# Four transposes of a graph network moved from TensorE to VectorE, a scratch tensor and DMA, and the weights loaded in four groups

## The reference, cut to what matters

```python
# layer 0
h1, h2, h3 = x @ W1, x @ W2, x @ W3
e = leaky_relu(h1 @ h2.T, 0.2); e = where(adj > 0, e, NEG)
x = layernorm(x + relu(softmax(e) @ h3))
# layer 1
h = x @ W; e = leaky_relu(h@a1 [:, None] + h@a2 [None, :]); e = where(adj > 0, e, NEG)
x = layernorm(x + elu(softmax(e) @ h))
# layer 2: a perceptron, an unmasked attention ("mixing"), a perceptron, a masked attention ("hand")
out = relu(x @ mlp1_w + mlp1_b)                     # 512 wide
out = elu(elu(softmax(f1[:, None] + f2[None, :]) @ h_fc)) + out
out = relu(out @ mlp2_w + mlp2_b)                   # 256 wide, the mixed output "o3"
out = relu(elu(elu(attention(out, adj, W_hand, a_hand))) + out)
x = layernorm(x + out)
# layer 3: four heads, adjacency mask
x = layernorm(x + (softmax(mask(q @ k.T / 8)) @ v) @ wo.T + bo)
```

## Time and profile before

| | |
|---|---|
| median of 3 runs | 2919.27 us (2908.69 to 2920.22) |
| the profiled execution, its own time | 2918.28 us |
| its span, first to last instruction | 2916.5 us |
| PE, PEld, DVE, ACT, POOL busy, share of the span | 92, 87, 78, 69, 53% |
| mean granted TensorE clock | 0.983 of full |
| instructions | 61536 |

### The profile page before, as it was taken

One profiled execution on the slowest core, in us unless ns is written; L12 is line 12 of the kernel. 1 busy time (PEld: TensorE's weight loads), 2 busy tenths in 40 slices (PEclk: granted clock), 3 DMA queues, 4 the chain that ended last, 5 costly groups with the idle time before them and its releaser, 6 DMA issues.

```text
span 2916.5 us, 61536 instructions
## 1 busy us (share of the span) xinstructions
PE 2689.4 (92%) x22472; PEld 2551.3 (87%) x22472; DVE 2278.2 (78%) x6124; ACT 1998.7 (69%) x4801; POOL 1556.0 (53%) x2119
## 2 busy tenths in 40 slices
PE   4689999999999999999999999999999999999974
PEld 4589999999999999998999998999999999998863
DVE  3257888888888888888888887888888888888874
ACT  1357777777777776777777777777777777776752
POOL 0235555555555555555556555555655555555542
PEclk9799999999999999999999999999999999999997
DMA  3001222222122122212212221221222122122222
GB/s 109 19 16 37 77 81 64 57 81 80 41 80 81 59 63 80 74 47 81 80 51 71 81 72 49 81 81 48 74 81 70 52 80 80 41 81 73 66 66 73
DMA packets 132766, 195.17 MB, mean 67 GB/s; under 512 B 14832, under 2 KB 97136, under 8 KB 132464
## 3 DMA queue, kind: packets, MB, share of 16 engines
q1 hardware_dynamic: 132464, 191.24, 22.7%
HBM read 107.30 MB, written 83.89 MB: 66 GB/s over the span
## 4 chain that ended last, share of the span: by engine, by line
PE 60%; DMA 13%; ACT 8%; SPq 8%; DVE 6%; issue 4%; POOL 1%; POOLq 0%; DVEq 0%
PE ps L224 29%; DMA p4T<-scratch 10%; PE ps L378 6%; SPq L208 6%; PE ps L240 5%; PE ps L436 4%; PE ps L337 4%; PE ps L233 3%; PE ps L338 3%; DMA scratch<-p 3%; DVE p L950 3%; PE ps L456 2%; ACT p L671 2%; PE ps L360 2%; DVE h_lo L692 1%
## 5 line engine op out<-in xcount | busy, mean ns | idle before, releaser
L1067 POOL TENSOR_TENSOR p<-p,rd 128x512 f32<-128x512 f32 x256 | 269.8, 1054 | 20.0
L671 ACT ACTIVATE p<-p,nmx 128x256 f32<-128x256 f32 x512 | 255.7, 504 | 25.4 <-DVE nmx L935 25.2
L991 POOL TENSOR_TENSOR o1Tp_lo<-o1T,o1Tp_hi 128x1024 fp32r<-128x1024 f32 x64 | 153.8, 2403 | 220.8 <-ACT o1Tp_hi L472 220.8
L1003 POOL TENSOR_SCALAR xn<-act,nmean,rstd 128x256 f32<-128x256 f32 x384 | 243.6, 643 | 18.3 <-POOL rstd L998 11.2
L456 PE MATMUL ps<-p4T,v 128*64 128x256 f32 x1024 | 144.3, 404 | 118.2 <-DMA p4T<-scratch 117.7
L995 POOL TENSOR_TENSOR vare<-mv,eps 128x2 f32<-128x2 f32 x256 | 108.0, 422 | 270.5 <-DVE mv L748 270.5
L1060 POOL TENSOR_TENSOR rd<-some,den 128x2 f32<-128x2 f32 x256 | 53.5, 209 | 354.6 <-DVE den L944 354.6
L456 PEld LDWEIGHTS ps<-p4T,v 128*64 128x64 f32 x1024 | 67.3, 140 | 178.1 <-DMA p4T<-scratch 96.5
L692 DVE TENSOR_TENSOR xnT_lo<-ps,xnT_hi 128x512 fp32r<-128x512 f32 x192 | 132.1, 688 | 114.2 <-ACT xnT_hi L472 114.2
L935 DVE CUSTOM_DVE_ANT_0 p<-ps,mask 128x256 f32<-128x256 f32 x512 | 189.9, 418 | 33.3 <-PE ps L436 33.3
L480 ACT ACTIVATE sco<-sco,nmax 128x256 f32<-128x256 f32 x384 | 191.0, 500 | 28.9 <-DVE nmax L736 28.9
(11 more groups left out here) (248 smaller groups left out, 12683.1 us busy)
## 6 DMA issues: line engine op xcount, KB each, us to landing
scratch<-p SPq DMA_DIRECT2D x128, 512.0 KB, 2.9
p4T<-scratch SPq DMA_DIRECT2D x512, 128.0 KB, 3.9
x0T<-in_xT SPq DMA_DIRECT2D x64, 256.0 KB, 4.6
x<-in_x SPq DMA_DIRECT2D x64, 256.0 KB, 3.7
out<-xn SPq DMA_DIRECT2D x64, 256.0 KB, 3.0
o1T<-in_mlp SPq DMA_DIRECT2D x1, 512.0 KB, 4.4
p<-in_mlp SPq DMA_DIRECT2D x1, 512.0 KB, 4.5
att<-in_fc SPq DMA_DIRECT2D x1, 512.0 KB, 5.4
```

Of the source, the lines that this page charges most:

```text
L671: ins = nc.scalar.activation(rows_, rows_, ACT.Exp, scale=-1.0, bias=nmx4[:, h, m:m + 1], accum_out=den4[:, h, m:m + 1])
L991: return G.tensor_tensor(lo, whole, hi.bitcast(fp32), ALU.subtract)
L1003: ins = G.tensor_scalar(xn[:, m, :], y[:, m, :], nmean[i][:, m:m + 1], rstd[i][:, m:m + 1], ALU.add, ALU.mult)
L1067: G.tensor_tensor(rows_, rows_, rd4[:, h, :].unsqueeze(2).unsqueeze(3).broadcast_to([P, NT, QUADS, CT * QP]), ALU.mult).then_inc(S["p4n"], 1)
```

## The change

- **Turns.** `t0`, `t1`, `t3` and `o3` leave TensorE. DVE transposes 32 by 32 blocks of the tile (`turn`, `V.transpose`, 128x512) into `act[i]` (or `sco[2]` for the mixed output), SP writes it to a scratch tensor (one DMA of 256 KB, packets of 2 KB) and reads it back with four DMAs of 64 KB (packets of 512 B). ACT then makes the high part and POOL the low part from SBUF, in a block order (`high_of_turned`, `low_of_turned`). `r3` adds the turned mixed output from SBUF in two instructions.
- **Column sums.** `d2` has a stationary of 128 columns of ones, so the sums stand in every partition at once: 4 matmuls of 256 columns. DVE takes the reciprocal of 256 columns straight to `rdb`. The two spreading transposes and ACT's copy go.
- **Scores of layers 1 and 3** are written by ACT to SBUF (`sco`) and not to PSUM; DVE masks them there. `pfc` likewise.
- `n4` moves from DVE to POOL, with one `xn3` buffer instead of two. PSUM banks are handed over by a table of tenants.
- **Loads** come in four groups. Only W1, W2, W3, the first x and adj stand ahead of the first product; the splitting of the other weights is called from `run` on DVE just before the first use.
- The five lists of `ORDERS` are new, their highest stage is 8 instead of 9; `l0` is in stage 0 instead of 1.

```diff
@@ ORDERS (pe, first entries and the part around a4; the others are new as well)
-    "pe": "h3:8 a0:3 v4:9 f3:8 x0:5 g0:2 s40:9 d2:7 x1:6 t3:8 s42:9 v2:7 a3:8 m2:6 h0:2 b2:7 n2:6 o3:8 w2:7 s0:2 h1:5 c2:6 f1:5 t0:2 a4:9 r2:6 t1:5 ...",
+    "pe": "g0:0 c2:4 a1:3 h1:2 r2:4 a3:6 a0:1 f2:4 f1:2 a4:7 m3:5 y4:7 x1:3 h0:0 x3:6 m2:3 s0:0 q4:6 k4:6 h3:5 n2:3 v4:6 f3:5 d2:4 s40:6 v2:4 w2:4 s42:6 x0:1",
+    "sp": "i42:8 o5:6 o1:3 lt:0 i1:3 o0:1 i5:6 o3:6 st:8 i0:1 i3:6 o40:7 lx:1 o42:7 i40:7",
@@ sync
+            def pro_out(i):
+                def step(t):
+                    sp.wait_ge(S[f"pro{i}_x"], t + 1)
+                    wait(sp, S[f"pro{i}_dma"], back(t - 1))
+                    sp.dma_start(scratch_pro[i].rearrange("p w n -> p (w n)"), flat(act[i])).then_inc(S[f"pro{i}_dma"], 16)
+            def pro_in(i):
+                def step(t):
+                    sp.wait_ge(S[f"pro{i}_dma"], sent(t))
+                    for w in range(QUADS):
+                        sp.dma_start(rows_[w * QP:(w + 1) * QP, :, :], scratch_pro[i][:, w, :].rearrange("(q j) n -> j q n", q=QUADS)).then_inc(...)
@@ tensor
-            def t0(t):
-                pe.wait_ge(S["pro0"], t + 1)
-                transposes(bank[0], sco[0]).then_inc(S["proT0_mm"], 1)
             def d2(t):
                 pe.wait_ge(S["pfcl"], t + 1)
-                for m in range(NT):
-                    for k in range(NT):
-                        for i in (1, 0):
-                            ins = nc.tensor.matmul(ps[:, 5, 2 * m:2 * m + 2], pfcp[i][:, k, m * P:(m + 1) * P], ones2[:, :], ...
+                enter(5, "rdb", t + 1)
+                for k in range(NT):
+                    for i in (1, 0):
+                        ins = nc.tensor.matmul(ps[:, 5, 0:N], ones2[:, :], pfcp[i][:, k, :], ...
-            def b2(t):
-                pe.wait_ge(S["rdc"], t + 1)
-                spread(ps[:, 5, N:2 * N], lambda m: rdc[:, m:m + 1]).then_inc(S["b2_mm"], 1)
@@ scalar
             def t0(t):
-                ac.wait_ge(S["proT0_mm"], t + 1)
-                copy(proT[0][0][:, :, :], bank[0]).then_inc(S["proT0h"], 1)
+                ac.wait_ge(S["pro0_dma"], back(t))
+                wait(ac, S["av0_mm"], t)
+                high_of_turned(proT[0], 0).then_inc(S["proT0h"], 1)
@@ vector
+            def turn(i):
+                blocks = sco[i][:, :, :, :].rearrange("p b a n -> p (b a) n").rearrange("p c (w j) -> p w c j", w=QUADS)
+                return V.transpose(flat(act[i]).rearrange("p (w c j) -> p w c j", w=QUADS, j=QP), blocks)
             def t0(t):
-                dv.wait_ge(S["proT0h"], t + 1)
-                low_part(proT[0], bank[0]).then_inc(S["proT0"], 1)
+                dv.wait_ge(S["pro0"], t + 1)
+                wait(dv, S["xn0"], t)
+                turn(0).then_inc(S["pro0_x"], 1)
             def d2(t):
                 dv.wait_ge(S["d2_mm"], t + 1)
-                V.reciprocal(rdc[:, :], ps[:, 5, 0:4:2]).then_inc(S["rdc"], 1)
+                wait(dv, S["att"], t)
+                V.reciprocal(rdb[:, :], ps[:, 5, 0:N]).then_inc(S["rdb"], 1)
@@ gpsimd
+            def t0(t):
+                po.wait_ge(S["proT0h"], t + 1)
+                low_of_turned(proT[0], 0).then_inc(S["proT0"], 1)
```

561 lines of the change are left out of this document (335 added, 226 removed), and 8 rows, old and new, of the table ORDERS.

## The result

The changed kernel takes **2988.11 us** (median of 4 runs, 2986.22 to 2990.06), the kernel before 2916.61 us in the same session (2908.69 to 2920.22). The ratio is 1.0232 with a 95% interval of 1.0205 to 1.0259: 2.3% slower, where 3.4% faster was forecast.

A forecast was written before the change was run, and what follows sets the result against it. PE was taken as the bound: 38.67 us of work plus 2.4 of wait, 41.1 a round. 14.5 + 245 + 55 x 41.1 + 299 = 2819 us, plus 1.8 outside the span: 2820 us; 8 in 10 from 2725 to 2905.

The forecast's parts named there:

- Neither binds: Claim that DVE, at 36.8 us in a round of 41.1, and POOL, at 29.6, would not limit the kernel.
- What the others gain: Work on engines other than PE per round: DVE 35.1 to 39.5 us, taken as 36.8; ACT near 31; POOL 29.6.
- my upper bound of 39.5: Most DVE work expected per round, with SBUF inputs costing 3.0 us and the wide reciprocal adding 1.65.
- The upper bound, 1.8 us: Longest time expected for DVE's 256-column reciprocal, charging 5.5 ns per column; the lower bound was 0.43 us.
- The sentence on the Trainium skill's eight repeats: On DVE's wide reciprocal: iterative divide, repeat count 8; if paid per column 2.1 us, with PE's wait near 3.4.
- The wait of a4: PE's wait for read-back probabilities, 1.54 us a round before, was to become 2.4 us.
- my lowest sum of 1.75: PE's wait at a4 in us a round if nothing else, such as the wide reciprocal, is late.
- What TensorE loses: Eighteen transposes (1.98 us) and cheaper column sums (0.43) save 2.41 us a round; PE's own work falls to 38.67.
- The ends: Outside full rounds: first products at 14.5 us instead of 43.0, filling 245 instead of 221, draining 299 instead of 307.8.
- SP is not a bound: A rival had SP's in-order DMA issues delaying a4: 43.5 us a round, 2967 us if issues average 1.3; chance 0.10.
- DVE takes over: Rival: DVE's upper costs meet, 39.5 us of work, round 42.5 us, 2920 us in all; chance 0.08.

The follow-up runs named there:

- x11_all_low_short: Changed kernel with GpSimd's low parts of the three turned tiles, o1T and o3T cut to 2 columns, the rest zeros: 2802.4 us, ratio 0.960.
- x2_scores_psum: Changed kernel with ACT writing the scores of layers 1 and 3 to PSUM as before and DVE masking them there: 2853.4 us, ratio 0.978.
- x3_both: Changed kernel with those scores in PSUM and the wide reciprocal replaced by multiplication with a constant, division left out: 2843.2 us, ratio 0.974.
- x12_elu_hidden_first: Changed kernel with scores in PSUM, narrow column sums, and a1 ahead of j2 and r2 ahead of z2 on DVE: 2822.6 us, ratio 0.967.
- the first three experiments: Changed kernel with the wide reciprocal replaced by a constant multiplication, with scores in PSUM, and with both edits: 2847.6, 2853.4 and 2843.2 us.
- x8_loads_first: Changed kernel with all weights loaded ahead of the first product, their splitting left where the change put it: 3006.3 us, ratio 1.030.
- x9_before_wide_sums: Kernel before with wide column sums and the 256-column reciprocal on DVE, without spreading transposes and ACT's copy: 2927.5 us, ratio 1.004.
- x6_pool_short: Changed kernel with GpSimd's low parts of the three turned tiles cut to 2 columns, the rest zeros: 2962.9 us, ratio 1.015.

## Why the prediction was wrong

The span was forecast at 2819 us and was 2988.3. The sum by its own terms: the ninth start was to be at 14.5 + 245 = 259.5 and was at 251.7 (-8); 55 rounds of 41.1 were 55 of 44.04 (+162); the drain was 314 instead of 299 (+15). The step that failed is the length of a round. DVE was to have room in a round of 41.1 us ("Neither binds"), and PE's wait was to be 2.4 us a round, all of it `a4`. PE waited 4.40, of which 4.2 for DVE. The parts:

- **"What the others gain" is where the error lies.** It priced an instruction with both inputs in SBUF at 0 to 0.43 us for its inputs, from the 1096 ns of `L902` in the earlier trace rows. That row was itself a mean of held instructions, as its shortest, median and longest show, and an occurrence of the kernel before:

```profile
L902 DVE SCALAR_TENSOR_TENSOR act<-act,xn x64: 681/1050/1953, 212.9 to 2868.3; 128x512 f32<-128x512 f32 x64
...
1531.72 2.40 POOL L991 TENSOR_TENSOR o1Tp_lo<-o1T,o1Tp_hi 128x1024 fp32r<-128x1024 f32 x1 [3.11 <-ACT o1Tp_hi L472]
1533.63 1.04 DVE L902 SCALAR_TENSOR_TENSOR act<-act,xn 128x512 f32<-128x512 f32 x1
```

  The same instruction takes 682 ns in the changed kernel. That is within 2% of the 671 ns with one input in PSUM, so two SBUF inputs cost next to nothing by themselves, and the price is what GpSimd does at that moment. The four maskings exceed the PSUM form by 0.72 us each. The prediction also priced only the new instructions. The old ones, `att<-ex,att`, `o2T_lo` and `att<-att,o1T`, grew by 0.54, 0.75 and 0.36, one beside a new low part and two beside old work that the new order puts there. Together that is 4 x 0.72 + 1.65 = 4.5 us a round, where I had some 1 us in the middle value, less the 0.41 that `L902` gained. DVE came to 40.3 us a round, above my upper bound of 39.5. `x11_all_low_short` shows the cause for the maskings: with GpSimd's instructions short, the same masking takes 405 ns.
- **The reciprocal was mis-sized.** The upper bound, 1.8 us, was right (1.757) and the middle was taken. It is (1757 - 150) / 254 = 6.3 ns per further column. It matters less by itself than by what it pushes: with the scores in PSUM (`x2_scores_psum` against `x3_both`), leaving it out gives only 0.2 us a round. The sentence on the Trainium skill's eight repeats (VectorE: DVE Perf Modes, First, the fixed hardware budget) had the right sign, paid per column; its estimate of 2.1 us is 0.3 too long by this trace.
- **"The wait of a4" did not come.** 2.4 us a round was forecast, 0.17 came. My reckoning asked when the data would be there, and not whether PE would be; PE, held 4.2 us a round elsewhere, came to `a4` late. When DVE is relieved the wait appears, at 1.01 (`x11_all_low_short`) and 1.18 us (`x12_elu_hidden_first`), below my lowest sum of 1.75. So the chain to `p4T` was laid out a little too long besides.
- **"What TensorE loses" was right, at full clock.** 38.67 us of own work was forecast. With the wide sums and a clock of 1.00 it is 38.96 to 38.99 (round less waits, in the first three experiments), 0.3 more. The changed kernel has 39.64 at 0.98, about 0.7 more a round. That the waits are what lowered the clock was not tested.
- **"The ends"** came out 8 us too long at the start and 15 too short at the end. The 245 us of filling do not follow from their terms: 221 + 28 less four times 2.4 is 240. Loading in groups is worth 18 us (`x8_loads_first`).
- **SP is not a bound.** The read-backs land in 2.0 us where I assumed 3.9, and PE waits for none of them except `p4T`:

```profile
scratch_pro<-act SPq DMA_DIRECT2D x192, 256.0 KB, 2.1
sco<-scratch_pro SPq DMA_DIRECT2D x768, 64.0 KB, 2.0
```

The rival that came true is "DVE takes over", to which I gave 0.08 because both of its bounds would have to hold. They are not independent: the reciprocal decides whether the masking of step 3 meets GpSimd. The measured time lies beyond its 2920, since its bound for the SBUF inputs was not one.

What stays open: how much of the loss of `x9_before_wide_sums` is the clock; no run holds the clock fixed. The four turns, the new lists and the new table of banks were never taken back or tried one by one, so what each is worth is not known. PE's waits for `nmx` and for the elu are waits to enter a bank that DVE has not left, and whether another bank for `s42` or `a3` would have hidden them was not tried.

## What to carry to other kernels

An instruction of VectorE with both inputs in SBUF has its own duration only while GpSimd is idle; beside a GpSimd instruction it lasts as long as that one does, and its own time comes behind. A mean hides this; the shortest, the median and the longest of a group show it. So before work goes to GpSimd, or an operand from PSUM to SBUF, lay both engines' lists side by side and look at what they will meet, including the instructions that are not edited and the old work that a new order moves. A new operation on an engine with room to spare costs what its successors run into, and it is tested by taking away what they run into. And a forecast wait for data must ask of both sides: when the data comes, and when the engine does.

## What the runs showed of the hardware

- A masking of 256 columns beside a GpSimd subtraction ended 0.28 to 0.30 us after it in the occurrences that I followed, whether it had been held 0.15 or 2.0 us, and took some 410 ns alone; from PSUM it was never over 426 ns in the changed kernel. The longer ones end behind GpSimd by their own time less some 0.13 us as well: `att<-ex,att` 1.09 us after `proT_lo` (1.22 alone), `L902` 0.55 after `o1Tp_lo` (0.68 alone). The transpose of 128x512 (0.70 us, at most 0.71) and the subtractions from PSUM (at most 0.69) were not held.
- An instruction with a single SBUF input can be held too: `ex<-ex` took 1334 ns instead of 724 in `x6_pool_short`, where it starts inside a multiplication of GpSimd on `p` (at 1525.66 us, in one that runs from 1525.43 to 1526.47).
- GpSimd is held as well: its product of 2 columns took 542 ns in the mean of the changed kernel and 196 in `x9_before_wide_sums`. In `x6_pool_short` one that starts at 1527.76 us, inside `att<-att,o1T` (1527.61 to 1528.81), takes 1.10 us and ends 0.05 after it.
- The reciprocal on VectorE costs 6.3 ns per further column (150 ns for 2, 1757 for 256), a transpose in a row on TensorE 0.11 us, and a switch of ScalarE's function tables 1283 ns. The Trainium skill, ScalarE activation tables: per-element evaluation and per-set limits, What a function is on this engine, states that figure for two functions in different sets, and the trace has it to the nanosecond.
